# The last four tiles' sums of a mixture-of-experts layer: own buffers, shared expert first, three of eight terms added on the tensor engine

## The reference, cut to what matters

```
x = x + attention(layernorm(x))                  # 16 heads, 4 key/value heads, rotary
h = layernorm(x)
topv, topi = top_k(h @ gate_w.T, 8)              # 64 experts, 8 for each token
rw = softmax(topv)
out = sum over the 8 chosen experts e of
      rw[e] * ((silu(h @ gate[e]) * (h @ up[e])) @ down[e])
shared = (silu(h @ sh_gate.T) * (h @ sh_up.T)) @ sh_down.T
x = x + out + sigmoid(h @ sh_gate1.T) * shared
```

## Time and profile before

| | us |
|---|---|
| median of 3 runs (lowest, highest) | 1220.87 (1215.87, 1222.19) |
| profiled execution, device time | 1212.77 |
| its span, first to last instruction | 1211.0 |
| PE busy | 1023.7 (85%) |
| DVE busy | 710.7 (59%) |
| ACT busy | 676.3 (56%) |
| POOL busy | 723.8 (60%) |

### The profile page before, as it was taken

The page is one execution under the profiler, slowest core; times in us unless marked ns, Lnnn a source line. Parts: engine busy times, 40 slices in busy tenths (PEclk is TensorE's granted clock), DMA queues, the critical chain, the costliest instruction groups (busy, mean ns, idle before and its releaser), DMA issues. The chain is left out here.

```text
span 1211.0 us, 24260 instructions
## 1 busy us (share of the span) xinstructions
PE 1023.7 (85%) x7378; PEld 809.7 (67%) x7378; DVE 710.7 (59%) x2229; ACT 676.3 (56%) x1650; POOL 723.8 (60%) x954
## 2 busy tenths in 40 slices
PE   2799989899989898898998611999999999999962
PEld 1466666666666666666665401999989889999950
DVE  2466776767767677777674550222236656666666
ACT  2366665666656656666554101777656667766630
POOL 3111122774856847658367775577777777777770
PEclk9689999999999999999898855999999999999985
DMA  2388876821312313212132994777778989998735
GB/s 89 131 261 278 270 250 209 285 100 44 112 56 80 118 32 110 83 58 97 39 133 81 323 321 155 217 220 219 219 265 313 374 307 339 316 357 282 260 111 187
DMA packets 142157, 233.23 MB, mean 193 GB/s; under 512 B 17271, under 2 KB 119878, under 8 KB 136656
## 3 DMA queue, kind: packets, MB, share of 16 engines
q1 hardware_dynamic: 67216, 101.06, 25.8%
q0 software_dynamic: 27648, 69.28, 15.8%
q10 hardware_dynamic: 47168, 61.35, 15.3%
HBM read 107.32 MB, written 132.66 MB: 198 GB/s over the span
## 5 line engine op out<-in xcount | busy, mean ns | idle before, releaser
L1363 POOL DMA_INDIRECT res_d<-y,dst_i x320 | 321.6, 1005 | 111.0 <-issue 82.8
L453 POOL DMA_INDIRECT rows_d<-pay,slot_i x256 | 258.4, 1009 | 73.4 <-issue 67.8
L858 DVE TENSOR_REDUCE nmax<-ps 128x1 f32<-128x512 f32 (+3 forms) x448 | 225.6, 530 | 103.7 <-PE ps L508 101.8
L724 ACT ACTIVATE wgu_s<-ps 128x512 f32<-128x512 f32 x320 | 191.3, 599 | 108.2 <-PE ps L508 105.0
L508 PE MATMUL ps<-mask,ident_b 128*128 128x256 bf16 (+1 forms) x640 | 172.2, 269 | 0.0
L501 PE MATMUL ps<-kT,qT 96*128 96x512 f32 (+3 forms) x512 | 166.8, 388 | 6.2 <-DVE nmax L858 4.0
L1294 PE MATMUL psB<-wgu_s,xT 128*128 x1280 | 171.9, 278 | 0.0
L1311 PE MATMUL psD<-wdp_s,innerT 128*128 x640 | 165.7, 382 | 3.7 <-ACT innerT L1199 2.5
L548 PE MATMUL ps<-qT,kT 128*128 128x512 f32 (+3 forms) x512 | 161.3, 377 | 0.9 <-ACT qT L737 0.6
L1294 PEld LDWEIGHTS psB<-wgu_s,xT 128*128 128x128 f32 x1280 | 158.2, 195 | 0.4 <-issue 0.4
L1118 DVE TENSOR_TENSOR inner<-inner,psB 128x128 f32<-128x128 f32 x160 | 45.7, 286 | 188.9 <-ACT inner L1193 185.6
(11 more groups left out here) (241 smaller groups left out, 1622.3 us busy)
## 6 DMA issues: line engine op xcount, KB each, us to landing
rows_d<-blank ACTq DMA_DIRECT2D x8, 5440.0 KB, 19.4
xg<-rows_d SPq DMA_DIRECT2D x160, 272.0 KB
yk<-res_d SPq DMA_DIRECT2D x32, 1024.0 KB
wgu_s<-wgu_in ACTq DMA_DIRECT2D x8, 1024.0 KB, 13.5
xs<-x_d SPq DMA_DIRECT2D x32, 192.5 KB
x_d<-x SPq DMA_DIRECT2D x30, 192.5 KB, 2.5
res_d<-y,dst_i POOLq DMA_INDIRECT x320
wgu_s<-x_in SPq DMA_DIRECT2D x32, 128.0 KB, 2.1
```

Source lines behind the costliest of these rows:

```text
L453: pool.indirect_dma_start(rows_d, bass.IndirectOffsetOnAxis(ap=slot_i[par][:, t, k:k + 1], axis=0), pay[par][:, t, :], None).then_inc(s_sc ...
L724: act.activation(pexp[p % 4][:, s, :], ps2[:, (5 * p + s) % 2, :], ACT.Exp, scale=HEAD_D ** -0.5).then_inc(s_exp, 1)
L858: return dve.tensor_reduce(nmax[u][:, tile, heads[0]:heads[-1] + 1], src, AX.X, ALU.max, negate=True)
L1363: pool.indirect_dma_start(res_d, bass.IndirectOffsetOnAxis(ap=dst_i[:, j % (2 * G):j % (2 * G) + 1], axis=0), y[:, j % Y, :], None, bounds ...
```

## The change

Nothing changes in the attention or in the work of the blocks. In the tiles' work:

- The loop has three more steps (`STEPS` = 170), so tile 27's sum is now in the loop, at steps 164 to 169, and `late_sums` is tiles 28 to 31.
- Tiles 30 and 31 get places of their own for `yk` and `xs`, in the space of `wgu_s`, which no one reads once the last gate and up product is done (`e_b_ps` at `PAIRS`). Tiles 28 and 29 keep the two old buffers. Each late load has its own semaphore (`l_xs`, `l_yk`).
- SP loads the late tiles' `xs` first (30, 31, 28, 29), then waits for all 320 scatters, then issues the four loads of `yk` in a row.
- Behind the loop DVE writes 12 diagonal matrices (128x128, the identity times a routing weight of each token), for terms 5, 6 and 7 of the four tiles, also into `wgu_s`.
- The shared expert of all four late tiles comes before any of their sums. Tiles 30 and 31 use PSUM of `psA`.
- For the late tiles DVE adds terms 0 to 4 only. PE adds terms 5 to 7 on top of the shared expert's result in PSUM: three products of a diagonal with a term of `yk`, accumulated. `mix` adds both.

```
--- before.py
+++ after.py
@@ -1009,11 +1009,14 @@
             c_in = [sem(f"yk_in{k}") for k in range(2)]
             c_out = [sem(f"fin_out{k}") for k in range(2)]
             c_acc = [sem(f"sum_step{k}") for k in range(2)]
+            l_xs = [sem(f"late_rows_in{k}") for k in range(TILES)]
+            l_yk = [sem(f"late_terms_in{k}") for k in range(TILES)]
+            l_diag, l_down = sem("diagonals_ready"), sem("late_shared_down")
...
-            STEPS = PAIRS + DOWN + 1
+            STEPS = PAIRS + DOWN + 4
...
-            shared_bank = [(sum_step(tile) if tile not in late_sums else tile) % 2 for tile in range(ALL_TILES)]
+            assert late_sums == list(range(ALL_TILES - TILES, ALL_TILES))
+            LATE, ON_PE = late_sums[0], 3
+            shared_bank = [(sum_step(tile) if tile < LATE else tile) % 2 for tile in range(ALL_TILES)]
+            def space(at, rows, width):
+                return wgu_s[:, at:at + rows * width].rearrange("p (a b) -> p a b", b=width)
+            def yk_at(tile):
+                return yk[:, tile % 2] if tile < LATE + 2 else space((tile - LATE - 2) * TOP * D, TOP, D)
+            def xs_at(tile):
+                if tile < LATE + 2:
+                    return xs[:, tile % 2]
+                return space(2 * TOP * D + (tile - LATE - 2) * (D + SHARED), 1, D + SHARED)[:, 0]
+            def diag_at(tile, k):
+                return space(4 * TOP * D + (tile - LATE) * ON_PE * P, ON_PE, P)[:, k - TOP + ON_PE]
+            def shared_at(tile):
+                return psC[:, shared_bank[tile]] if tile < LATE + 2 else psA[:, tile % 2]
+            def added_before(tile):
+                return TOP * (tile // 2) - (ON_PE if tile >= LATE + 2 else 0)
+            def added(tile):
+                return TOP - ON_PE if tile >= LATE else TOP
...
@@ -1072,9 +1107,20 @@
                     while tile < ALL_TILES and load_turn(tile) <= j + 1:
                         load_tile(tile)
                         tile += 1
-                while tile < ALL_TILES:
+                while tile < LATE:
                     load_tile(tile)
                     tile += 1
+                for tile in (LATE + 2, LATE + 3, LATE, LATE + 1):
+                    if tile >= LATE + 2:
+                        sp.wait_ge(e_b_ps, PAIRS)
+                    else:
+                        sp.wait_ge(c_acc[tile % 2], TOP * (tile // 2))
+                        sp.wait_ge(c_sh, tile - 1)
+                    sp.dma_start(xs_at(tile), x2_v[tile]).then_inc(l_xs[tile - LATE], 16)
+                for n in range(Y):
+                    sp.wait_ge(e_out[n], 16 * ((BLOCKS - n + Y - 1) // Y))
+                for tile in late_sums:
+                    sp.dma_start(yk_at(tile).rearrange("p k h -> p (k h)"), res_v[tile]).then_inc(l_yk[tile - LATE], 16)
             @block.vector
             def _(dve):
@@ -1125,30 +1171,32 @@
                     if tile >= 2:
                         dve.wait_ge(c_t_ps, tile - 1)
...
                 def add(tile, k):
                     u = tile % 2
-                    if k == 0:
+                    if k == 0 and tile >= LATE:
+                        dve.wait_ge(l_xs[tile - LATE], 16)
+                        dve.wait_ge(l_yk[tile - LATE], 16)
+                    elif k == 0:
                         dve.wait_ge(c_in[u], 32 * (tile // 2 + 1))
                     else:
-                        dve.wait_ge(c_acc[u], TOP * (tile // 2) + k)
+                        dve.wait_ge(c_acc[u], added_before(tile) + k)
                     at = tile * TOP + k
-                    dve.scalar_tensor_tensor(out=acc[:, u], in0=yk[:, u, k], scalar=rw_all[:, at:at + 1],
-                                             in1=xs[:, u, 0:D] if k == 0 else acc[:, u],
+                    dve.scalar_tensor_tensor(out=acc[:, u], in0=yk_at(tile)[:, k], scalar=rw_all[:, at:at + 1],
+                                             in1=xs_at(tile)[:, 0:D] if k == 0 else acc[:, u],
                                              op0=ALU.mult, op1=ALU.add).then_inc(c_acc[u], 1)
                 def mix(tile):
                     u = tile % 2
-                    dve.wait_ge(c_acc[u], TOP * (tile // 2 + 1))
+                    dve.wait_ge(c_acc[u], added_before(tile) + added(tile))
                     dve.wait_ge(c_y_ps, tile + 1)
-                    step = STEPS if tile in late_sums else sum_step(tile) + DOWN_SHARED
-                    dve.wait_ge(e_c, min(PAIRS, step - TURN + 1))
+                    if tile < LATE:
+                        dve.wait_ge(e_c, min(PAIRS, sum_step(tile) + DOWN_SHARED - TURN + 1))
                     if tile >= 2:
                         dve.wait_ge(c_out[u], 16 * (tile // 2))
-                    dve.tensor_tensor(fin[:, u], psC[:, shared_bank[tile], 2 * P:2 * P + D], acc[:, u],
+                    dve.tensor_tensor(fin[:, u], shared_at(tile)[:, 2 * P:2 * P + D], acc[:, u],
                                       ALU.add).then_inc(c_mix, 1)
...
+                dve.wait_ge(e_b_ps, PAIRS)
+                for tile in late_sums:
+                    for k in range(TOP - ON_PE, TOP):
+                        at = tile * TOP + k
+                        last = dve.tensor_scalar(diag_at(tile, k), ident, rw_all[:, at:at + 1], None, ALU.mult)
+                last.then_inc(l_diag, 1)
                 for tile in late_sums:
                     shared(tile)
-                    for k in range(TOP):
+                for tile in late_sums:
+                    for k in range(added(tile)):
                         add(tile, k)
                     mix(tile)
@@ -1207,18 +1262,24 @@
                 def shared(tile):
                     u = tile % 2
-                    act.wait_ge(c_in[u], 32 * (tile // 2 + 1))
+                    if tile >= LATE:
+                        act.wait_ge(l_xs[tile - LATE], 16)
+                    else:
+                        act.wait_ge(c_in[u], 32 * (tile // 2 + 1))
                     if tile >= 2:
                         act.wait_ge(c_sh, tile - 1)
...
                 def shT_copy(tile):
                     u = tile % 2
                     act.wait_ge(c_t_ps, tile + 1)
-                    if tile >= 2:
+                    if tile >= LATE + 2:
+                        act.wait_ge(l_down, tile - LATE - 1)
+                    elif tile >= 2:
                         act.wait_ge(c_y_ps, tile - 1)
-                    act.copy(shT[:, u], psC[:, shared_bank[tile], 2 * P:3 * P]).then_inc(c_t, 1)
+                    act.copy(shT[:, u], shared_at(tile)[:, 2 * P:3 * P]).then_inc(c_t, 1)
...
+                while stored < LATE:
+                    store(stored)
+                    stored += 1
                 for tile in late_sums:
                     shared(tile)
                     shT_copy(tile)
-                    while stored < tile:
-                        store(stored)
-                        stored += 1
                 while stored < ALL_TILES:
                     store(stored)
                     stored += 1
@@ -1314,12 +1375,12 @@
                 def turn_shared(tile):
                     pe.wait_ge(c_sh, tile + 1)
-                    pe.transpose(psC[:, shared_bank[tile], 2 * P:3 * P], sh[:, tile % 2, :], ident).then_inc(c_t_ps, 1)
+                    pe.transpose(shared_at(tile)[:, 2 * P:3 * P], sh[:, tile % 2, :], ident).then_inc(c_t_ps, 1)
                 def down_shared(tile):
                     pe.wait_ge(c_t, tile + 1)
-                    pe.matmul(psC[:, shared_bank[tile], 2 * P:2 * P + D], shT[:, tile % 2, :], shd_w[:],
-                              start=True, stop=True).then_inc(c_y_ps, 1)
+                    pe.matmul(shared_at(tile)[:, 2 * P:2 * P + D], shT[:, tile % 2, :], shd_w[:],
+                              start=True, stop=tile < LATE).then_inc(c_y_ps if tile < LATE else l_down, 1)
...
+                pe.wait_ge(c_mix, LATE)
+                pe.wait_ge(e_c, PAIRS)
+                pe.wait_ge(e_a, PAIRS)
                 for tile in late_sums:
-                    pe.wait_ge(c_mix, tile if tile == late_sums[0] else tile - 1)
                     turn_shared(tile)
                     down_shared(tile)
+                pe.wait_ge(l_diag, 1)
+                for tile in late_sums:
+                    pe.wait_ge(l_yk[tile - LATE], 16)
+                    for k in range(TOP - ON_PE, TOP):
+                        last = pe.matmul(shared_at(tile)[:, 2 * P:2 * P + D], diag_at(tile, k), yk_at(tile)[:, k],
+                                         start=False, stop=k == TOP - 1)
+                    last.then_inc(c_y_ps, 1)
             @block.gpsimd
             def _(pool):
```

More of the change, by code:

```diff
@@ L1127, in shared @@
                     dve.scalar_tensor_tensor(out=sh[:, u, 0:INNER], in0=act_s[:, u], scalar=half_t[:, u],
-                                             in1=xs[:, u, D + INNER + 1:D + SHARED],
+                                             in1=xs_at(tile)[:, D + INNER + 1:D + SHARED],
```

(10 more changed lines are left out.)

## The result

| | before | after |
|---|---|---|
| median of 18 runs each (lowest, highest), us | 1215.98 (1211.89, 1229.77) | 1210.05 (1204.5, 1216.12) |
| ratio after / before, 95% interval | | 0.9946 (0.9922 to 0.997) |
| span of the profiled execution, us | 1211.0 | 1202.9 |
| last scatter's start to the end of the span ("tail"), us | 29.7 | 21.7 |

The account below looks back on a forecast made before the run. POOL's row of scatters sets the blocks' end, then about 26 us of serial work. Terms put the last `mix` at 1201.25 against 1208.76, 7.5 us less: 1220.87 becomes 1213.4 us, range 1209.0 to 1219.0.

Parts of the forecast that it names:

- Start of the late loads: Late `yk` loads wait for 320 scatters, not 319: first issue at 1183.66, a loss of 1.29 us.
- Tile 28's landing: Tile 28's load without `xs` beside it saves 0.55 us, so it lands at 1188.39, bounds 1187.9 and 1188.94.
- The next landings: Loads of tiles 29 to 31 land 2.8 to 2.9 us apart, each a little before DVE is ready.
- DVE a tile: Five adds and `mix` per late tile take 3.02 us in place of 4.59; four tiles 12.08.
- PE: Three term products per late tile take 2.96 us at 1.2 GHz; the first `mix` waits 0.43.
- Diagonals: 12 diagonal writes on DVE behind tile 27's `mix` take 1.6 us (up to 5.0), hidden by POOL's last three scatters.
- POOL: Scatters starting beside DVE's diagonals are delayed 0 to 0.5 us, taken as 0.3, which moves the loads.
- Tile 27 in the loop: Tile 27's sum moved into the loop's last steps, with some 8 us of cover on ACT: costed at 0.
- 1 (diagonals hold POOL off): POOL gets no turn beside the diagonals and loses up to 3.4 us: gain 4.4, time 1216.5; chance 0.10.
- 2 (PE the bound): PE's late-tile products take 3.66 us a tile, end 2.6 later: gain 4.9, time 1216.0; chance 0.10.
- 3 (landings together): The four late loads share the engines and all land late, at 1196.6: no gain, 1220.9; chance 0.06.
- 4 (the loads held behind tile 29's `xs`): In SP's queue `yk` loads wait for tile 27's eighth add; slower, above 1227, if it ends after 1197; chance 0.04.

Follow-up runs that it names:

- e2: The kernel after, with the late loads waiting for 319 scatters and not 320: tail 20.4 us, ratio to before 0.9936.
- e3: The kernel after with all eight terms on DVE, no diagonals and no products for terms on PE: tail 27.4 us, ratio to before 0.9961.
- e5: The kernel after with five terms on PE and three on DVE: tail 20.9 us, ratio to before 0.9958.
- e12: As e10, but each late tile's four diagonals stand behind that tile's part of the shared expert on DVE: tail 19.5 us, ratio to before 0.9978.
- e9: The kernel after with 319 scatters, four terms on PE, tile 28's terms in two loads, own `fin` buffers for tiles 30 and 31: tail 23.3 us, ratio 0.9943.
- e8: The kernel after with 24 extra unused identity copies on DVE ahead of the diagonals, beside the last scatters: tail 22.8 us.
- e1: The kernel before with three more loop steps, so tile 27's sum is in the loop, nothing else: tail 29.4 us, ratio to before 0.9985.
- e10: As e9, plus unread PE products ahead of and inside the shared experts to keep PE busy: tail 22.6 us, ratio to before 0.9947.

## Why the prediction was right, step by step

- *Start of the late loads*, +1.29: the issue at 1183.66 was met to the hundredth, and e2 shows the price in full. The hundredth is luck: the last scatter started 0.09 us sooner and landed as much later, and with the landing of e3 the issue would have been 0.27 us earlier.
- *Tile 28's landing*: 1188.39 forecast, and 1183.66 + 4.73 in the chain of after is the same.
- *The next landings*: 2.8 to 2.9 us forecast, 2.49 measured. The rate was read from a stretch with two issues 1.2 us apart and a store among them. It did not matter: DVE was the bound either way.
- *DVE a tile*: 3.02 forecast, 2.93 measured, since the next tile's first add starts 0.34 us into the `mix`, where I had put it behind. 0.3 us over four tiles.
- *PE*: 2.96 for tile 28 forecast; from 1188.52 to 1191.44 it took 2.91, and the wait was 0.47 for 0.43. That PE would stay at 1.2 GHz was wrong from 1191.5 on and without effect at three terms; at five it decides (e5).
- *Diagonals*: 2.66 us, not 1.6. I took the copies' pace, and the product with a routing weight has 0.22 each (0.196 in e12). The cover held, but with 0.9 us left (PE's last shared product ends at 1187.52) and not 1.4, and e9 shows what it costs without.
- *POOL*, 0.3 us: did not come. The earlier trace rows gave a delay that neither e8's copies nor after's diagonals brought about; what delayed that scatter in the attention is open. The long scatters of the blocks' loop stand beside the sums (e8 above), so the row that the term was priced from does not stand for the diagonals. The Trainium skill ("SBUF — State Buffer", section "Who interferes with whom") says of a copy in a two-port mode and a GpSimd instruction that the one that comes second blocks fully. No scatter beside these copies shows it; the copies' own steps of up to 0.30 us are the only waiting there. Whether they ran in such a mode no run tells.
- *Tile 27 in the loop*, 0: e1 agrees.
- *Rivals.* 1 (diagonals hold POOL off) fell: one step of 1.36 us, the others 1.29. 2 (PE the bound) is real only from five terms on. 3 (landings together) fell: 2.49 us apart, in order. 4 (the loads held behind tile 29's `xs`): its issue was through by about 1177, well ahead of 1183.66; in e10 that wait ended beside the last scatter, and the loads still went out 1.4 us behind it.

The sum erred by 0.6 us in 8.1. Nearly all of it are two terms, 0.3 for POOL that did not come and 0.3 for DVE's pace; the small ones had both signs. The mechanism was the one forecast, part by part. That 1210.05 lies inside the range owes something to chance all the same: the range hung on a median of before that was 4.9 us too high, and 7.5 us off the later median would be 1208.5, below its lower end of 1209.0.

## What to carry to other kernels

Behind a loop that ends in a wait for DRAM, ask for each remaining step whether it needs the last data; what does not (here the shared expert, the rows, the diagonals) goes ahead of the wait, and is free only for as long as the engines reach it that much earlier, so its cover is to be stated as a number. Moving part of a serial chain from one engine to another pays for as long as the tiles behind win back what the second engine's first piece costs more at the low clock: here up to four terms of eight, and no longer at five. And take a part of the change out before believing its name: own buffers were worth 2.2 us, the terms on PE 5.7, each from one profile.

## What the runs showed of the hardware

- Four DMAs of 1.05 MB issued 0.4 us apart on one queue landed in order, 2.49 us apart, 425 GB/s.
- In after, PE's granted clock was 0.50 through the shared experts (1180.1 to 1187.5), in which PE was busy 5.9 of 7.4 us, and 1.00 from 1191.5 on, behind 3.1 us of the terms' products in which it was busy 2.98.
- 24 fp32 copies of 128x128 on DVE beside three indirect DMAs of POOL slowed none of them (0.99 us each). The copies start 0.135 us apart, as the casts of the earlier trace rows do, but once 0.18 and once 0.26 to 0.30 at each scatter, 0.162 in the mean.
- All 194 of 4480 scatters that took over 1.15 us (most take 0.99) overlapped an add or a `mix` of DVE.
